# Graph attention and two transformer layers: projections on four quadrants of TensorE, values as the moving operand in the first turn, and key-value products computed one stage earlier

## The chip, the cores and the metric

The kernel runs on one core of one Trainium2 chip, all in fp32. The metric is the device time of one execution in microseconds (us); lower is better.

## What is computed

The input x has 32 sequences of 64 tokens with 256 features, and ctx has the same shape. Four blocks follow each other on x:

```python
# block 0 (cross attention over channels; C = 64 rows of a sequence)
q, k   = w_qk @ x, w_qk @ y              # y = ctx
energy = q_T_k                           # features x features, softmax, scaled by column sums
x      = x + relu(w_t @ (x - x_v @ attention) + b_t)
# blocks 1 and 2 (a transformer layer with 16 heads of 16)
h = layernorm(x); x = x + self_attention(h, mask) @ w_ao
h = layernorm(x); x = x + cross_attention(h, ctx, cross_mask) @ w_co
h = layernorm(x); x = x + gelu(h @ w1) @ w2
# block 3 (an RWKV-like layer: data-dependent mixing, decay, a recurrence
# over 64 tokens with 8x8 states per head, group norm, and a gated feed-forward)
```

In the attention of a layer, scores are masked, the row maximum is subtracted, exp is taken, and the product with the values is divided by the row's sum.

## The kernel before

Everything is in SBUF as 128-partition tiles, two sequences to a tile of tokens, and 4 groups of 4 such tiles. Each engine has its own instruction queue, written out in order by hand, and waits on semaphores. There are four parts.

**The gate stage** (`phase_a`, block 0) loops over 16 tiles of two sequences. On TensorE a step for tile t is `energy` of tile t+2 (L362), `project` of t+3, `turn_back` (L387), `read_out` of t+1 (L377) and `mix_out` (L393). `project` makes q and k of both sequences with a block-diagonal 128x128 weight: L348 for y (k's side), L349 for x, each 256 columns, into one PSUM bank, then the x-values by L352 into another. ScalarE's `copy_qk` (L439) copies q and k out when L349 is done; VectorE's `values` (L502) adds the bias to the x-values. SP loads x and y of a tile as two DMAs (`load`, L272 and L273). Its queue is in order: four reloads, four stores (L285), four reloads, and so on; a store waits for POOL's `add` (L330).

**The layers** (`phase_b`) are 8 turns, 4 groups times 2 layers. Turn 0 is written by `first_turn`, turns 1 to 6 are one loop over `turn`, and turn 7 is `last_turn`. Each turn has 8 attention tiles k (4 self, 4 cross) and in between the MLP of the turn before (`hidden` L1112, `pre`, `gelu` L1454, `mlp_out` L1126) and the entry projections of the turn after (`queries_in`, `keys_in`, both L944; `values_in`, L954). Turn 0 has no MLP of a turn before. One tile goes so:

- `scores` (PE, L1050) -> `mask` (DVE, L1715) -> `add_mask` (POOL, L788) -> `maximum` (DVE, L1722) -> `subtract` (DVE, L1727) -> `exps` (ACT, L1423)
- `probs_T` (PE, L1060, 8 transposes) -> `copy_pT` (ACT, L1428) -> `times_v` (PE, L1074): values are the stationary operand (32 columns, a pair of heads), probabilities move (64 columns); the result has heads' features in the partitions
- `row_sums` (DVE: a reduction over 1024 elements, L1733, and a reciprocal, L1735) -> `widen` (ACT, L1433) -> `inv_T` (PE, L1082, 2 transposes) -> `copy_inv` (ACT, L1438) -> `normalize` (DVE, L1740), which multiplies the product by the transposed 1/sum
- `out_project` (PE, L1095) -> `residual` (DVE, L1749 to L1756) -> `inv_std` (POOL, L793) -> `norm` (DVE, L1761)

The scores live in two buffers, so tile k+2 is masked after tile k's transposes. `cross_masks` (DVE, L1706 and L1707) prepares the cross mask and `norm_in` (DVE, L1689) the next turn's input once a turn.

**The last MLP with the recurrence's head** (`last_mlp_first_head`) runs the MLP of turn 7 together with block 3's projections for its first group: mixing, decay, k, v, r, g, and k and v turned to tokens (`to_tokens`). VectorE computes the key-value products of the first half of the features there (`key_value`, L2421, four instructions).

**Block 3** (`phase_c`) starts with `recurrence()`: 16 scans on VectorE (L3402), each followed by a product on POOL (L2612) and sums on TensorE, with the four key-value products of the second half of the features (L3392) between the first scans. `bonus` (PE, L2810) and `own_value` (DVE, L3407) give the diagonal term. Three periods and a last one follow.

```python
FIRST_PE, FIRST_DVE = {0: "b", 6: "n", 12: "l0 l1"}, {0: "k0", 1: "k1", 2: "k2", 3: "k3", 4: "b", 13: "s"}
```

says what stands behind which scan: `k0` to `k3` the products, `b` the diagonal term, `s` the next group's token shift.

## Time and profile before

| | |
|---|---|
| three runs | 1069.5, 1066.68, 1068.3 us; median 1068.3 |
| profiled execution | 1070.31 us, its span 1068.5 us, mean TensorE clock 0.981 |
| busy in the span | PE 983.8 (92%), DVE 837.1 (78%), ACT 558.6 (52%), POOL 435.6 (41%) |
| DMA | 41.10 MB, mean 38 GB/s |

Times inside the kernel are counted from the start of the span. PE is TensorE, DVE VectorE, ACT ScalarE, POOL GpSimd, SP the queue that issues the DMAs. A matmul in fp32 is two instructions in the profile. A merged row of the timeline gives the start of its first instruction and the time to the end of its last one, which can lie beside the next row's start. The gate stage ends at 96.7 us, turn 0 at about 178, turn 6 at about 658, turn 7 at 726.6, and block 3 begins at 792.5.

### The profile page before, as it was taken

To read this page: it belongs to the slowest core of one execution; us is meant where nothing else is said; L and a number is where in the kernel's file an instruction comes from. 1 tells how busy PE (TensorE), PEld (TensorE's weight loads), DVE (VectorE), ACT (ScalarE), POOL (GpSimd) and SP (SyncE) were. 2 spreads that over 40 slices of the span, in tenths; PEclk is the share of its full clock that TensorE was granted. 3 is DMA by queue.
4 is the path that set the end of the run, shared out by engine and by line. 5 is a ranking of instruction groups with operands and counts; after the bars stand their busy time and mean duration, and the time that the engine had idled before them with its cause. 6 is when DMAs were issued, how large, how long until landed. Compare 5 with 4: busy or idle time off the path is not lost. (4 is left out here: it accounts for less than half of the span.)

```text
span 1068.5 us, 24715 instructions
## 1 busy us (share of the span) xinstructions
PE 983.8 (92%) x9328; PEld 660.3 (62%) x9328; DVE 837.1 (78%) x1591; ACT 558.6 (52%) x1088; POOL 435.6 (41%) x383
## 2 busy tenths in 40 slices
PE   7998688999999999999999999998986988989877
PEld 5775566677677677677677677674552453554535
DVE  3775999977977877877977978785368898997965
ACT  4663464683683683683683783743412534415332
POOL 2112445434443444434444444342326527365250
PEclk9999999999999999999999999999998999999988
DMA  8230100000001002013000000030010010010010
GB/s 265 82 104 29 47 1 22 26 21 22 26 21 62 26 21 71 25 37 101 26 21 22 26 21 21 2 136 21 1 40 24 1 40 22 0 40 3 1 40 20
DMA packets 38003, 41.10 MB, mean 38 GB/s; under 512 B 8640, under 2 KB 33536, under 8 KB 37648
## 3 DMA queue, kind: packets, MB, share of 16 engines
q1 hardware_dynamic: 37776, 39.54, 11.7%
q8 instruction: 79, 1.29, 0.5%
q14 instruction: 20, 0.16, 0.0%
q0 software_dynamic: 128, 0.10, 0.0%
HBM read 31.25 MB, written 8.39 MB: 37 GB/s over the span
## 5 line engine op out<-in xcount | busy, mean ns | idle before, releaser
L788 POOL TENSOR_TENSOR head_area<-head_area,b_self_add 128x1024 f32<-128x1024 f32 x32 | 84.5, 2641 | 123.1 <-DVE head_area L1715 123.1
L2612 POOL TENSOR_TENSOR c_rs<-c_st,head_area 128x512 f32<-128x512 f32 x64 | 83.7, 1335 | 98.6 <-DVE c_st L3402 97.0
L788 POOL TENSOR_TENSOR head_area<-head_area 128x1024 f32<-128x1024 f32 x32 | 76.8, 2399 | 87.0 <-DVE head_area L1715 87.0
L1112 PE MATMUL ps<-b_hT_mlp,wl 128*128 128x512 f32 x224 | 105.6, 599 | 0.0
L1126 PE MATMUL ps<-w,b_act_g 128*128 128x256 f32 x448 | 102.9, 383 | 0.3 <-ACT b_act_g L1454 0.3
L1423 ACT ACTIVATE head_area<-head_area 128x1024 f32<-128x1024 f32 x64 | 68.0, 1063 | 51.9 <-DVE head_area L1727 51.8
L793 POOL TENSOR_TENSOR b_rstd<-b_var,minus_half 128x1 f32<-128x1 f32 x63 | 36.3, 577 | 142.8 <-DVE b_var L1756 142.8
L1126 PEld LDWEIGHTS ps<-w,b_act_g 128*128 128x128 f32 x448 | 82.8, 190 | 13.8 <-issue 2.2
L944 PE MATMUL ps<-head_area,wl 128*128 128x512 f32 x176 | 85.1, 607 | 3.1 <-DVE area L1698 2.5
L1428 ACT ACTIVATE head_area<-ps 128x512 f32<-128x512 f32 x128 | 69.3, 599 | 33.4 <-PE ps L1060 33.3
L1722 DVE TENSOR_REDUCE b_neg_max<-head_area 128x16 f32<-128x1024 f32 x64 | 77.7, 1213 | 11.5 <-POOL head_area L788 10.8
L1727 DVE TENSOR_TENSOR head_area<-head_area,b_neg_max 128x1024 f32<-128x1024 f32 x64 | 78.0, 1219 | 0.8
L1733 DVE TENSOR_REDUCE b_inv_sum<-head_area 128x16 f32<-128x1024 f32 x64 | 77.6, 1212 | 0.5 <-ACT head_area L1423 0.4
L3402 DVE TENSOR_TENSOR_SCAN c_st<-head_area,ps 128x512 f32<-128x512 f32 x64 | 73.4, 1202 | 2.6 <-ACT ps L3105 2.5
L1095 PE MATMUL ps<-wl,b_cT 128*128 128x256 f32 x252 | 68.2, 393 | 4.0 <-issue 2.4
L1060 PE MATMUL ps<-ident,head_area 128*128 128x128 f32 x512 | 66.9, 274 | 3.5 <-ACT head_area L1423 2.3
L1060 PEld LDWEIGHTS ps<-ident,head_area 128*128 128x128 f32 x512 | 58.4, 141 | 18.0 <-issue 12.4
L954 PE MATMUL ps<-wl,head_area 128*64 128x128 f32 x1024 | 64.2, 283 | 0.0
L954 PEld LDWEIGHTS ps<-wl,head_area 128*64 128x64 f32 x1024 | 58.4, 142 | 5.7 <-issue 4.8
L1112 PEld LDWEIGHTS ps<-b_hT_mlp,wl 128*128 128x128 f32 x224 | 39.7, 190 | 35.8 <-issue 35.1
L1438 ACT ACTIVATE head_area<-ps 128x256 f32<-128x256 f32 x64 | 24.4, 381 | 69.9 <-PE ps L1082 69.9
L1095 PEld LDWEIGHTS ps<-wl,b_cT 128*128 128x128 f32 x252 | 43.4, 189 | 14.1 <-issue 6.8
(294 smaller groups left out, 2153.0 us busy)
## 6 DMA issues: line engine op xcount, KB each, us to landing
head_area<-x_mid SPq DMA_DIRECT2D x9, 512.0 KB, 3.8
wl<-in_wl SPq DMA_DIRECT2D x4, 1024.0 KB, 6.4
head_area<-in_ctxT SPq DMA_DIRECT2D x8, 512.0 KB, 4.2
x_mid<-b_x_out SPq DMA_DIRECT2D x8, 512.0 KB, 3.5
area<-in_wc SPq DMA_DIRECT2D x1, 2336.0 KB, 8.3
a_x_in<-in_x SPq DMA_DIRECT2D x16, 128.0 KB, 2.8
a_y_in<-in_ctx SPq DMA_DIRECT2D x16, 128.0 KB, 3.5
w<-in_w SPq DMA_DIRECT2D x2, 1024.0 KB, 9.2
```

What stands on the lines that cost most here:

```text
L788: pool.tensor_tensor(t, t, m.unsqueeze(1).broadcast_to([P, NH, S]), ALU.add).then_inc(add_ok, 1)
L944: mm = pe.matmul(ps[:, YB + c, :], weight(name, k, first + c * P, first + (c + 1) * P), rhs[:, k, :], start=(k == 0), stop=(k == NC - 1))
L954: mm = pe.matmul(ps[odd * S:(odd + 1) * S, YB + half, b * P:(b + 1) * P], lhs[:, k, t:t + S], weight(name, k, odd * P, (odd + 1) * P), sta ...
L1060: mm = pe.transpose(ps[:, PT + half, i * P:(i + 1) * P], sc[:, k % 2, half, 2 * i:2 * i + 2, :].rearrange("q i k -> q (i k)"), w["ident"][ ...
L1095: mm = pe.matmul(ps[:, CO, OUT], cT[:, half, p * P:(p + 1) * P], weight(("ao", "co")[a], half), start=(half == 0), stop=(half == 1))
L1112: mm = pe.matmul(ps[:, YB + j % 2, :], weight("w1", k, j * P, (j + 1) * P), hT_mlp[:, k, :], start=(k == 0), stop=(k == NC - 1))
L1126: mm = pe.matmul(ps[:, YB + MLP_BANK[p], 0:D], act_g[:, j, p * P:(p + 1) * P], w["w2"][:, j, :], start=(j == 0), stop=(j == NJ - 1))
L1722: dve.tensor_reduce(neg_max[:, k % 2, :], t, AX, ALU.max, negate=True).then_inc(max_ok, 1)
L1727: dve.tensor_tensor(t, t, neg_max[:, k % 2, :].unsqueeze(2).broadcast_to([P, 2 * NPAIR, S]), ALU.add).then_inc(sub_ok, 1)
L1733: dve.tensor_reduce(inv_sum[:, k % 2, :], t, AX, ALU.add).then_inc(inv_ok, 1)
L2612: pool.tensor_tensor(rs[:, i % BUFS, :], st[:, i % 3, :], rF[:, i // RS, :], ALU.mult).then_inc(rs_ok, 1)
L3402: dve.tensor_tensor_scan(st[:, i % 3, :], decay[:, i // RS, :, :].rearrange("f b t -> f (b t)"), ps[:, VB[i % 4], :], 0.0, ALU.mult, ALU.a ...
```

## The change

Three parts. In the gate stage, `project` does four 64x64 matmuls of 256 columns, one for each quadrant of the array, q into the second half of the x-values' bank and k into the other bank. A quadrant off the diagonal takes sequence 1 to the partitions of sequence 0 and back, so y is loaded with its two sequences exchanged, in two DMAs. `copy_qk` waits for the x-values too, and `values` for `copy_qk`.

```diff
-                sp.dma_start(y_in[:, p, :], y).then_inc(ld_xy[p], 16)
+                for side in range(2):
+                    sp.dma_start(y_in[(1 - side) * S:(2 - side) * S, p, :], y[side * S:(side + 1) * S, :]).then_inc(ld_xy[p], 16)
...
-                pe.wait_ge(ld_xy[p], 32 // NP * (t - p) + 32)
+                pe.wait_ge(ld_xy[p], 48 // NP * (t - p) + 48)
                 after(pe, qk_ok, t)
-                pe.matmul(ps[:, PROJ, 0:D], w0[:, 0, :], y_in[:, p, :], start=True, stop=True)
-                pe.matmul(ps[:, PROJ, D:2 * D], w0[:, 0, :], x_in[:, p, :], start=True, stop=True).then_inc(proj_ps, 1)
                 after(pe, xvb_ok, t)
+                pe.sem_inc(proj_go, 1)
+                for side in range(2):
+                    h, other = slice(side * S, (side + 1) * S), slice((1 - side) * S, (2 - side) * S)
+                    pe.matmul(ps[h, XV, D:2 * D], w0[h, 0, h], x_in[h, p, :], start=True, stop=True)
+                    pe.matmul(ps[other, PROJ, 0:D], w0[h, 0, h], y_in[h, p, :], start=True, stop=True)
...
-                act.wait_ge(proj_ps, t + 1)
+                act.wait_ge(xv_ps, t + 1)
...
                 dve.wait_ge(xv_ps, t + 1)
+                dve.wait_ge(qk_ok, t + 1)
```

In turn 0 the probabilities become the stationary operand (64 columns) and the values move. The values of a pair of heads get two columns of ones (`VW = HD + 1`, set by four small memsets on POOL), so that the product brings the row sums with it. VectorE takes 1/sum of 16 columns and multiplies; the result, with tokens in the partitions, is transposed by `first_result_T` and copied by `first_copy_cT`. `row_sums`, `widen`, `copy_inv` and `normalize` are gone in turn 0; the later turns keep them.

```diff
+            def first_times_v(n, k):
...
+                    for i in range(NPAIR // 2):
+                        j = half * NPAIR // 2 + i
+                        for b in range(2):
+                            q = slice(b * S, (b + 1) * S)
+                            mm = pe.matmul(ps[q, CX, j * 2 * VW:(j + 1) * 2 * VW], pT[:, half, i, q], vP[a][:, 2 * p + b, j, :],
+                                           start=True, stop=True)
...
+            def first_result_T(n, k):
+                pe.wait_ge(inv_ok, 2 * tile(n, k) + 2)
+                for half in range(2):
+                    f = slice(half * P, (half + 1) * P)
+                    mm = pe.transpose(ps[:, CX, f], inv_wide[:, f], w["ident"][:, :])
...
+            def first_copy_cT(n, k):
+                p = k % NP
+                act.wait_ge(inv_ps, 2 * tile(n, k) + 2)
+                act.activation(cT[:, :, p * P:(p + 1) * P], ps[:, CX, CT].rearrange("f (h q) -> f h q", h=2), ACT.Copy).then_inc(c_ok, 1)
...
+            def first_normalize(n, k):
+                dve.wait_ge(inv_ps, 2 * tile(n, k) + 1)
+                pairs = ps[:, CX, 0:NH * VW].rearrange("q (j v) -> q j v", v=2 * VW)
+                inv = inv_sum[:, 0, :].rearrange("q (j o) -> q j o", o=2)
+                dve.reciprocal(inv, pairs[:, :, PW:2 * VW]).then_inc(inv_ok, 1)
+                dve.wait_ge(inv_ok, 2 * tile(n, k) + 1)
+                dve.tensor_tensor(inv_wide[:, :].rearrange("q (j o e) -> q j o e", o=2, e=HD), pairs[:, :, 0:PW].rearrange("q j (o e) -> q j o e", o=2),
+                                  inv.unsqueeze(3).broadcast_to([P, NPAIR, 2, HD]), ALU.mult).then_inc(inv_ok, 1)
```

With this the written orders of all three kinds of turn are new, on PE, ACT, DVE and POOL. In `turn` and `last_turn` nothing is added or removed. In turn 0, on VectorE, two tiles before and now (L1733 and L1735 are `row_sums`, L1740 `normalize`; L1764 is now `maximum`, L1769 `subtract`, L1757 `mask`, L1788 and L1790 `first_normalize`, L1799 to L1806 `residual`, L1811 `norm`). Before, tile 3's place:

```order
L1715 TENSOR_TENSOR head_area<-ps,head_area 128x1024
L1761 TENSOR_SCALAR b_xc<-b_x_cur,b_mv,b_rstd 128x256
L1733 TENSOR_REDUCE b_inv_sum<-head_area 128x16
L1735 RECIPROCAL b_inv_sum<-b_inv_sum 128x16
L1740 TENSOR_TENSOR b_cT<-ps,head_area 128x2x128
L1722 TENSOR_REDUCE b_neg_max<-head_area 128x16
L1727 TENSOR_TENSOR head_area<-head_area,b_neg_max 128x1024
```

and now, from `maximum(5)` to `maximum(7)`:

```order
L1764 TENSOR_REDUCE b_neg_max<-head_area 128x16
L1811 TENSOR_SCALAR b_xc<-b_x_cur,b_mv,b_rstd 128x256
L1769 TENSOR_TENSOR head_area<-head_area,b_neg_max 128x1024
L1788 RECIPROCAL b_inv_sum<-ps 128x16
L1790 TENSOR_TENSOR head_area<-ps,b_inv_sum 128x256
L1757 TENSOR_TENSOR head_area<-ps,head_area 128x1024
L1764 TENSOR_REDUCE b_neg_max<-head_area 128x16
L1769 TENSOR_TENSOR head_area<-head_area,b_neg_max 128x1024
L1757 TENSOR_TENSOR head_area<-ps,head_area 128x1024
L1788 RECIPROCAL b_inv_sum<-ps 128x16
L1790 TENSOR_TENSOR head_area<-ps,b_inv_sum 128x256
```

The reduction is gone, and a `mask` stands directly ahead of a `maximum`. `cross_masks` stood behind `mask(1)` and now stands behind `mask(3)`, and `norm_in` behind `mask(4)`.

In the middle turns, on ScalarE around the first gelu (L1423 and L1468 are `exps`, L1403 and L1448 `queries_in`, L1433 and L1478 `widen`, L1396 and L1441 `norm_out_mid`). Before:

```order
L1423 ACTIVATE head_area<-head_area 128x1024
L1433 ACTIVATE head_area<-b_inv_sum 128x256
L1403 ACTIVATE area<-ps,vl 128x512
L1454 ACT_TABLE_LOAD
L1454 ACTIVATE b_act_g<-b_act_g 128x2048
L1394 REGISTER_ALU
L1396 ACTIVATE head_area<-ps,vl 128x128 x2
```

and now:

```order
L1468 ACTIVATE head_area<-head_area 128x1024
L1504 ACT_TABLE_LOAD
L1504 ACTIVATE b_act_g<-b_act_g 128x2048
L1448 ACTIVATE area<-ps,vl 128x512
L1478 ACTIVATE head_area<-b_inv_sum 128x256
L1439 REGISTER_ALU
L1441 ACTIVATE head_area<-ps,vl 128x128 x2
```

The gelu moved ahead of `queries_in` and `widen`. On TensorE, `queries_mid(2)` moved from behind `probs_T(4)` to a place ahead of `keys_in(0)`, and `keys_ctx(0)` stands ahead of `last_project(0)` at the start of a turn. In turn 7, `hidden` and `mlp_out` are spread later: `mlp_out(3)` is now behind `inv_T(7)`.

The third part moves the four products of the second half of the features into the stage of the last MLP. Their buffer `kv2` then must be free before block 3: it shares the new tensor `early` with the layer weights that are no longer read by that time (`wl_early`, the first seven sets of columns; `wl_columns` finds the place).

```diff
-        FIRST_PE, FIRST_DVE = {0: "b", 6: "n", 12: "l0 l1"}, {0: "k0", 1: "k1", 2: "k2", 3: "k3", 4: "b", 13: "s"}
+        FIRST_PE, FIRST_DVE = {0: "b", 6: "n", 12: "l0 l1"}, {4: "b", 13: "s"}
...
-        kv = [kv1, sb("kv2", NP, RS * P)]
+        kv = [kv1, w["kv2"]]
...
+                key_value(0, 0)
+                key_value(0, 1)
+                key_value(0, 2)
+                key_value(0, 3)
+                next_norm()
+                key_value(1, 0)
+                key_value(1, 1)
                 own_weight()
-                next_norm()
                 result(0)
+                result(1)
+                key_value(1, 2)
+                key_value(1, 3)
                 gate()
-                result(1)
```

On VectorE, at the start of block 3, before (L3402 is the scan, L3392 the product):

```order
L3402 SCALAR_TENSOR_TENSOR c_st<-head_area,ps 128x512
L3392 TENSOR_TENSOR c_kv<-head_area 128x1024
L3402 SCALAR_TENSOR_TENSOR c_st<-head_area,ps 128x512
L3392 TENSOR_TENSOR c_kv<-head_area 128x1024
L3402 SCALAR_TENSOR_TENSOR c_st<-head_area,ps 128x512
L3407 TENSOR_TENSOR head_area<-ps,head_area 128x512 x2
L3402 SCALAR_TENSOR_TENSOR c_st<-head_area,ps 128x512 x9
```

and now, with the end of the stage ahead of it (L2462 is the product, L2408 `result`, L2438 `gate`, L3450 the scan):

```order
L2408 TENSOR_TENSOR b_x_out<-ps,b_x_mlp 128x256 x2
L2462 TENSOR_TENSOR early<-head_area 128x1024 x2
L2438 SCALAR_TENSOR_TENSOR head_area<-head_area,ps 128x512 x2
L2408 TENSOR_TENSOR b_x_out<-ps,b_x_mlp 128x256 x2
...
L3450 SCALAR_TENSOR_TENSOR c_st<-head_area,ps 128x512 x5
L3455 TENSOR_TENSOR head_area<-ps,head_area 128x512 x2
L3450 SCALAR_TENSOR_TENSOR c_st<-head_area,ps 128x512 x9
```

In the stage of the last MLP, TensorE's order changes too (`mlp_out(2)` goes behind the projections of r and g), and both gelus of ScalarE go behind the copies of k.

## Rows read from the trace of the kernel before

**Rows 1.** Busy time by stage: turn 0, a middle turn, turn 7, last MLP, recurrence
```profile
core 0: us, PE busy (x) PEld busy (x) DVE busy (x) ACT busy (x) POOL busy (x), PEclk, DMA share, GB/s
108.00:178.40 70.40, 55.00 (x829) 40.34 (x829) 65.12 (x118) 37.82 (x72) 37.44 (x31) 0.98 0.06 19
178.40:258.30 79.90, 79.41 (x919) 56.83 (x920) 66.42 (x130) 47.69 (x80) 34.37 (x30) 0.98 0.09 27
658.10:726.60 68.50, 64.89 (x766) 47.71 (x765) 57.80 (x118) 40.53 (x71) 26.23 (x24) 1.00 0.18 61
726.60:792.50 65.90, 61.52 (x200) 32.62 (x200) 29.76 (x60) 21.47 (x29) 14.48 (x14) 0.97 0.01 4
792.50:822.40 29.90, 19.18 (x103) 10.87 (x104) 28.76 (x28) 4.39 (x20) 23.00 (x16) 0.86 0.19 56
```
**Rows 2.** Timeline, gate stage, PE: start, us, instruction [idle before <-releaser]
```profile
41.75 1.14 PE L362 MATMUL ps<-a_qk 64*128 64x256 f32 x8
42.81 0.70 PE L348 MATMUL ps<-a_y_in,a_w 128*128 128x256 f32 x2
43.35 0.59 PE L349 MATMUL ps<-a_x_in,a_w 128*128 128x256 f32 x2
43.78 0.61 PE L352 MATMUL ps<-a_w,a_x_in 128*128 128x128 f32 x4
44.54 1.15 PE L377 MATMUL ps<-a_xv_n,a_att 128*64 128x65 f32 x32
46.25 1.14 PE L362 MATMUL ps<-a_qk 64*128 64x256 f32 x8
...
62.09 0.70 PE L348 MATMUL ps<-a_y_in,a_w 128*128 128x256 f32 x2 [1.21 <-DMA a_y_in<-in_ctx]
```
**Rows 3.** Timeline of the SP queue at tile 12, and L273's time to landing
```profile
58.30 0.43 SPq L273 DMA_DIRECT2D a_y_in<-in_ctx  x1
...
DMA to landing us min/median/max: 2.1/3.5/6.8
```
**Rows 4.** Timeline of DVE: turn 0, and L1707 in turn 0 and in turn 2
```profile
108.07 2.47 DVE L1707 TENSOR_SCALAR head_area<-head_area 128x256 f32<-128x256 f32 x1
...
144.38 1.21 DVE L1733 TENSOR_REDUCE b_inv_sum<-head_area 128x16 f32<-128x1024 f32 x1
145.62 0.25 DVE L1735 RECIPROCAL b_inv_sum<-b_inv_sum 128x16 f32<-128x16 f32 x1
...
273.73 0.29 DVE L1707 TENSOR_SCALAR head_area<-head_area 128x256 f32<-128x256 f32 x1
```
**Rows 5.** Timeline of PE in turn 0: `times_v` and `scores`
```profile
130.91 0.65 PE L1074 MATMUL ps<-head_area,area 128*32 128x64 f32 x32 [1.19 <-DVE b_cT L1740]
...
132.56 0.69 PE L1050 MATMUL ps<-head_area 32*64 32x128 f32 x32
```
**Rows 6.** Timeline of ACT, a middle turn: the first gelu
```profile
293.00 1.28 ACT L1454 ACT_TABLE_LOAD   x1
294.29 1.91 ACT L1454 ACTIVATE b_act_g<-b_act_g 128x2048 f32<-128x2048 f32 x1
```
**Rows 7.** Timeline of PE, end of turn 7
```profile
726.59 1.10 PE L2125 MATMUL ps<-wl,b_cT 128*128 128x256 f32 x4 [1.20 <-PEq L2036]
```
**Rows 8.** Timeline of DVE, stage of the last MLP: the four products
```profile
777.52 4.63 DVE L2421 TENSOR_TENSOR head_area<-head_area 128x1024 f32<-128x1024 f32 x4 [7.33 <-ACT head_area L2309]
```
**Rows 9.** Timeline of the recurrence: DVE, PE and POOL
```profile
794.71 1.20 DVE L3392 TENSOR_TENSOR c_kv<-head_area 128x1024 f32<-128x1024 f32 x1
795.83 1.22 DVE L3402 TENSOR_TENSOR_SCAN c_st<-head_area,ps 128x512 f32<-128x512 f32 x1
796.96 1.20 DVE L3392 TENSOR_TENSOR c_kv<-head_area 128x1024 f32<-128x1024 f32 x1
...
798.01 3.15 PE L2810 MATMUL ps<-head_area,area 128*128 128x512 f32 x4
...
806.16 11.55 POOL L2612 TENSOR_TENSOR c_rs<-c_st,head_area 128x512 f32<-128x512 f32 x9 [1.03 <-DVE c_st L3402]
```

More of the change, by code:

```diff
@@ new lines, in first_turn @@
+                queries_mid(n, 2)
+                norm_T_in(nxt, prev)
+                last_project(n, 4, prev)
+                probs_T(n, 4, nxt)
+                queries_in(nxt, 0)
+                first_times_v(n, 4)
+                next_scores(n, 4, nxt)
+                norm_T_mid(n, 3)
+                queries_in(nxt, 1)
+                first_result_T(n, 4)
+                probs_T(n, 5, nxt)
+                queries_mid(n, 3)
+                first_times_v(n, 5)
+                next_scores(n, 5, nxt)
@@ new lines, in first_turn, with last_turn @@
+                values_in(nxt, 1, prev)
+                first_result_T(n, 7)
+            def last_turn(n, prev, nxt):
+                keys_ctx(n, 0, prev)
+                probs_T(n, 0, nxt)
+                last_project(n, 0, prev)
+                times_v(n, 0)
+                next_scores(n, 0, nxt)
+                keys_ctx(n, 1, prev)
+                inv_T(n, 0)
+                values_ctx(n, 0)
+                last_project(n, 1, prev)
+                values_ctx(n, 1)
+                probs_T(n, 1, nxt)
@@ new lines, in turn @@
+                pre(prev, 4)
+                copy_inv(n, 2)
+                pre(prev, 5)
+                queries_mid(n, 1)
+                copy_pT(n, 3)
+                norm_out(0, nxt)
+                next_exps(n, 3, nxt)
+                gelu(prev, 0)
+                queries_in(nxt, 0)
+                widen(n, 3)
+                norm_out_mid(n, 2)
+                copy_inv(n, 3)
+                queries_in(nxt, 1)
+                queries_mid(n, 2)
+                copy_pT(n, 4)
+                next_exps(n, 4, nxt)
@@ new lines, in turn @@
+                keys(0, nxt, 0)
+                widen(n, 4)
+                copy_inv(n, 4)
+                norm_out_mid(n, 3)
+                keys(0, nxt, 1)
+                copy_pT(n, 5)
+                queries_mid(n, 3)
+                pre(prev, 6)
+                widen(n, 5)
+                pre(prev, 7)
+                next_exps(n, 5, nxt)
+                gelu(prev, 1)
+                copy_pT(n, 6)
+                widen(n, 6)
+                copy_inv(n, 5)
+                next_exps(n, 6, nxt)
@@ L1908, in first_turn @@
                 row_sums(n, 3)
+                norm_in(nxt if entry_of is None else entry_of)
                 normalize(n, 2)
```

841 lines of the change are left out of this document (391 added, 450 removed).

## The prediction

> **What bounds the kernel now.** I read the table of busy time by stage first [rows 1], then each engine's timeline inside a stage, since the page's average (PE 92%) mixes stages with different limits. A difference below 0.3% (3.2 us) can't be told from no change in a measurement of this kernel.
>
> In the gate stage (the first 96.7 us) TensorE works without a gap, 4.50 us a tile from one `energy` (L362) to the next, except where tile 12 waits 1.21 us for its y [rows 2]. In the first turn of the layers VectorE is busy for 65.12 of 70.40 us while TensorE is busy for 55.00 [rows 1]: VectorE sets the pace. In the six middle turns it is the reverse, TensorE 79.41 of 79.90, and the last turn is at 64.89 of 68.50. The stage that mixes the last MLP with the recurrence's head has TensorE at 61.52 of 65.90, VectorE at 29.76. In the recurrence VectorE is busy 28.76 of 29.90 us, TensorE 19.18. The later periods (246 us) are untouched by the diff.
>
> So a microsecond taken from VectorE counts in the first turn and in the recurrence, one taken from TensorE in the gate stage, and a new order of the middle turns can hardly win anything (0.5 us a turn) but can lose.
>
> **Part 1, quadrants.** Removed per tile: the two 128x128 by 256 matmuls L348 and L349, which take 0.97 us of TensorE (42.81 to 43.78) [rows 2]. Added: four 64x64 by 256. The price is not in the trace. From below, one 256-column matmul takes 0.43 us (L349, start to next start), and four quadrants that run side by side can't be faster. From above, `energy` has four 256-column matmuls on two halves of the array and takes 1.06 us to the next start. The nearest row is `scores` (L1050), which splits rows and columns both: sixteen matmuls of 128 columns on eight pieces, ideally 16 / 8 x 0.215 = 0.43 us, take 0.69 in their row, and about 0.16 of such a figure lies beside the next matmul (L349: 0.59 against 0.43) [rows 2, 5]. I take 0.60, so 0.37 us saved. The Trainium skill, "TensorEngine Tiling (Array Packing)", section Key Properties, says that a change of tiling mode drains TensorE, and the change adds one mode. The row bears on it: L348, behind a change of mode, takes 0.54 us to the next start and its twin L349 0.43, so a change costs 0.11 us, and that is inside the 0.60. Tiles 2 to 15 pay off, 14 x 0.37 = 5.2 us. The first two don't: ScalarE now copies q and k only after the x-values' matmuls too, which takes back what the quadrants save there.
>
> Against it stand the transfers. y comes as two DMAs, one more issue of 0.43 us on SP's queue, and the data lie there 2.1 us or more later [rows 3]. Ahead of the first matmul that is 0.5 us more. At tile 12 TensorE already waits; it arrives there 0.37 us earlier and y is complete up to 0.43 us later, so 0.8 us is lost. The reload of tile 8 has the same place behind the stores and starts without a gap only just, so 0.8 again. Sum of the part: 5.2 - 0.5 - 1.6 = **3.1 us faster**, bounds 6 (transfers don't matter) and 1 (the group takes 0.75).
>
> **Part 2, the first turn.** Per tile VectorE loses `row_sums`' reduction, 1.24 us from its start to the reciprocal's [rows 4]; the reciprocal and one multiply of 256 columns stay, with other operands. Eight tiles give 9.9 us of VectorE. ScalarE loses one small copy a tile, which is not on the path. How much of the 9.9 arrives? Three things stand in its place.
> First, TensorE: `first_times_v` has 16 matmuls with 64-column weights and 34 moving columns, where `times_v` (L1074) had 32-column weights and 64 moving columns, 0.65 us for its 32 instructions [rows 5]. The nearest row is L377, with 64-column weights too, 1.15 us for 32 [rows 2]. I take that, so 0.5 x 8 = 4 us more TensorE in a turn that has 15 us of slack.
> The Trainium skill, the same page, Instruction Overhead, states about 60 cycles for any short matmul; by that 34 columns would cost no more than 64 do, the 4 us would vanish, and the turn would be up to 2 us shorter.
> Second, the chain. Today 1/sum goes beside the transposes; now it waits for exp, transposes, copy and product, and then `first_result_T` and the copy of cT. With the order written in the diff, following VectorE's queue from row to row, the late maxima are hit: `mask(6)` is directly followed by `maximum(6)`, which needs POOL's mask in between (2.4 us).
> Third, `cross_masks` and `norm_in` now follow a `mask`, so that they run beside POOL's mask. What that costs is shown by L1707: 0.29 us alone, 2.47 us beside POOL [rows 4], some 2.2 us for each of the two. Today the 2.47 hides behind the wait for `maximum(1)`. The Trainium skill, "SBUF — State Buffer", explains such a pair as an exclusive lock on shared ports; the row agrees.
> I count 9.9 - 2.5 (exposed maximum, 2.4 and a start) - 2.2 (half of 4.4, the other half in idle time that the removal opens) - 1.2 (later residuals wait for the longer chain) = **4.0 us faster**, bounds 8 (only the maximum is exposed) and 1.
>
> **Part 3, middle and last turns.** No instruction is added or removed, only moved. A turn is 79.90 us long and TensorE fills it [rows 1]. I followed the new order by hand. The spot with least room is ScalarE's gelu: a table load and 1.91 us, 3.2 together [rows 6], now stand ahead of `queries_in`, `widen(3)` and `norm_out_mid(2)`, while TensorE's `queries_mid(2)` moved ahead of `probs_T(4)`. Behind `exps(4)` ScalarE then has 3.2 + 0.7 + 0.4 + 0.7 = 5.0 us of work, TensorE about 4.7 (transposes, two projections). That is a stall of 0 to 0.5 us a turn; against it keys_ctx now covers the turn's end. I take **0**, with 3 us loss and 1 us gain as bounds. In the last turn `mlp_out(3)` (3.5 us) moves behind the last `inv_T`, where TensorE idles 1.20 us now [rows 7]: **1 us faster**, bounds 3 and -1.
>
> **Part 4, products a stage ahead.** In the recurrence four key-value products of 1.12 us (794.71 to 795.83) leave VectorE [rows 9]: 4.5 us. Scans then follow each other at 1.13 us. POOL's product takes 1.28 us (11.55 / 9) and three buffers let it lag; with `own_value`'s 1.2 us and the shift's time between scans it catches up. TensorE's `bonus` (L2810, 3.15 us at the cold clock, first at 798.01) is gated by scan 1 and moves forward by about one product only, so `own_value` waits some 0.4 us. **4.1 us faster**, bounds 4.5 and 2.5. The products land in a stage where VectorE waits 7.33 us ahead of the first four [rows 8] and TensorE is the bound; eight products are 9 us. If the cover fails (values' tokens later than now), `result(3)` is late by at most 1.5 us; counted 0.
>
> **Sum.** 3.1 + 4.0 + 0 + 1 + 4.1 = 12.2 us off the profiled execution's 1070.31, whose span is 1068.5. The three runs have a median of 1068.3, 2.0 below it; taken off that, **1056 us**.
>
> **The rivals.**
> (a) *The first turn pays nearly in full and the transfers don't bite*: 8 instead of 4, 6 instead of 3.1, together 7 more: 1049. For it: the order was rewritten around the new durations. Against: the exposed maximum is in the order itself. 0.20.
> (b) *TensorE and the chain take the first turn back and the middle turns lose a little*: 1 instead of 4, and 0.5 us x 6: 1062. For it: TensorE's slack of 15 falls to 11 against 9.9 taken from VectorE, so both run near their limit. 0.18.
> (c) *Slower.* ScalarE's gelu block ends over 2 us after TensorE wants `queries_mid(2)`, in each of six turns. It decides from 12.2 / 6 = 2.0 us a turn; at 2.5 us it gives 1056 + 15 = 1071, at 3 us 1074. For it: TensorE has no slack to give there. Against: my count gives 0.5 at most. 0.05.
> (d) *The quadrants don't overlap* (they do not do what they say): four times 0.43 is 1.72 us, 0.75 more than today, x 14 = 10.5 slower in place of 3.1 faster: 1070, no change. Against: the rows of `energy` and `scores`, which overlap. 0.05.
> The forecast keeps 0.52.
>
> **Chances and range.** Forecast, (a) and (b) are faster by over 0.3% (below 1065.1); (d) is within 0.3%, (c) slower or just within. Faster 0.90, same 0.06, slower 0.04. The range takes in the bounds of the parts and half of (a): 1048 to 1063.
>
> **What would show it.** Tiles of the gate stage at 4.1 us, waits for y at tiles 8 and 12. In the first turn no L1733-like reduction, VectorE idle ahead of maximum(6), L1707's successor long beside POOL, the first middle turn some 7 us earlier. Middle turns at 79.9. Sixteen scans without a product between them, the recurrence's last `attention` 4 us nearer its start. The forecast is wrong if a tile stays at 4.5 us, if the middle period moves by over 0.5 us, or if VectorE's idle time in the first turn exceeds 10 us.

## The result, and the profile after

The changed kernel takes 1063.77 us in the median of 11 runs (1059.15 to 1066.76), the kernel before 1069.50 (11 runs, 1062.98 to 1075.45). The ratio is 0.9943, 95% interval [0.9924, 0.9963]: 4 to 8 us faster, and not the 12.2 that the sum had. A ratio is always the time over that of the kernel before, so below 1 is faster. The same kernel beside others later (`after_again`) had 1060.91 and 0.9917 [0.9894, 0.9940]. The profiled execution shown here took 1062.13 us, span 1060.2, where before had 1070.31 and 1068.5.

Busy time by stage of the kernel after: gate stage (to the first `scores`), first turn (to the second `probs_T` of turn 1, called its second transposes from here on), a middle turn, the last turn, last MLP, recurrence:

```profile
core 0: us, PE busy (x) PEld busy (x) DVE busy (x) ACT busy (x) POOL busy (x), PEclk, DMA share, GB/s
0.00:100.70 100.70, 80.56 (x922) 53.33 (x923) 57.83 (x151) 55.72 (x183) 21.06 (x32) 0.98 0.41 127
100.70:190.50 89.80, 79.26 (x1103) 61.18 (x1104) 72.99 (x135) 39.23 (x70) 42.54 (x35) 0.91 0.07 21
429.10:508.70 79.60, 79.08 (x930) 57.14 (x929) 65.74 (x128) 49.85 (x84) 35.71 (x29) 1.00 0.18 55
666.90:725.00 58.10, 56.05 (x624) 40.87 (x622) 46.66 (x98) 35.08 (x63) 21.69 (x20) 1.00 0.19 64
725.00:791.10 66.10, 61.67 (x200) 32.50 (x201) 33.51 (x64) 18.80 (x27) 14.54 (x14) 0.97 0.03 9
791.10:815.80 24.70, 16.64 (x103) 9.88 (x104) 23.57 (x23) 4.38 (x20) 18.69 (x15) 0.95 0.22 67
```

The same view of before, for the stretches that [rows 1] cut elsewhere:

```profile
0.00:96.70 96.70, 84.13 (x856) 61.89 (x856) 56.91 (x150) 56.26 (x183) 19.86 (x28) 1.00 0.42 132
96.70:188.00 91.30, 74.85 (x1102) 54.51 (x1103) 81.80 (x143) 42.31 (x78) 43.20 (x34) 0.94 0.07 21
666.00:726.60 60.60, 56.99 (x629) 41.64 (x627) 50.70 (x105) 36.12 (x64) 21.97 (x20) 1.00 0.20 66
792.50:821.70 29.20, 18.48 (x103) 10.66 (x104) 28.06 (x27) 4.39 (x20) 22.30 (x15) 0.87 0.19 58
```

Read the lengths in pairs. The recurrence is 4.5 us shorter and its VectorE lost just that (28.06 to 23.57). The last turn is 2.5 shorter. The first turn is 1.5 shorter although VectorE's busy time fell by 8.8 there, and TensorE's mean clock is lower (0.94 to 0.91). The gate stage is **4.0 us longer**, and its PE busy time fell with it: TensorE has less to do and waits. Who it waits for, in the gate stage of after:

```profile
PE ps L369 <- DMA a_y_in<-in_ctx: 5.1, 3, 2.4
PE ps L413 <- DVE a_diff L557: 2.8, 5, 1.1
PE ps L382 <- ACT a_qk L460: 2.7, 2, 2.0
```

and of before:

```profile
PE ps L393 <- DVE a_diff L535: 1.3, 4, 0.5
PE ps L348 <- DMA a_y_in<-in_ctx: 1.2, 1, 1.2
PE ps L362 <- ACT a_qk L439: 1.2, 1, 1.2
```

(total us, times, longest). The waits grew by 6.9 us: 3.9 for y, 1.5 for the copies of q and k, 1.5 for the difference. The longest is one that the prediction didn't have, at tile 4. TensorE's timeline of after at tile 4, and then a step without a wait:

```profile
27.62 0.40 PE L369 MATMUL ps<-a_x_in,a_w 64*64 64x256 f32 x1 [2.44 <-DMA a_y_in<-in_ctx]
28.24 1.23 PE L372 MATMUL ps<-a_w,a_x_in 128*128 128x128 f32 x4
29.82 1.93 PE L397 MATMUL ps<-a_xv_n,a_att 128*64 128x65 f32 x32
...
36.54 1.13 PE L382 MATMUL ps<-a_qk 64*128 64x256 f32 x8
37.60 0.43 PE L369 MATMUL ps<-a_x_in,a_w 64*64 64x256 f32 x1
38.20 0.71 PE L372 MATMUL ps<-a_w,a_x_in 128*128 128x128 f32 x4
38.74 0.38 PE L407 MATMUL ps<-ident,a_xr_t 128*128 128x128 f32 x2
...
40.77 1.14 PE L382 MATMUL ps<-a_qk 64*128 64x256 f32 x8
```

The quadrants do what they say: 37.60 to 38.20 is 0.60 us where the two matmuls took 0.97 [rows 2]. But L372 behind them now takes 0.54 to the next start, where L352 took 0.44, so a step is 4.23 us against 4.50: 0.27 saved, not 0.37. After the idle 2.44 us TensorE runs at its low clock: L397 takes 1.93 us there and 1.15 elsewhere.

SyncE's queue (start, us) shows why y is late. L284 and L272 load x, ahead of y. After:

```profile
1.74 1.18 SPq L286 DMA_DIRECT2D a_y_in<-in_ctx  x2
...
9.26 0.59 SPq L309 DMA_DIRECT2D early<-in_wl  x1
...
16.20 3.71 SPq L284 DMA_DIRECT2D a_x_in<-in_x  x1
20.01 1.16 SPq L286 DMA_DIRECT2D a_y_in<-in_ctx  x2
```

and before:

```profile
6.01 0.43 SPq L296 DMA_DIRECT2D wl<-in_wl  x1
...
14.18 3.22 SPq L272 DMA_DIRECT2D a_x_in<-in_x  x1
17.49 0.38 SPq L273 DMA_DIRECT2D a_y_in<-in_ctx  x1
```

A pair of issues holds the queue for 1.1 to 1.2 us. Four tiles push the first weights from 6.01 to 9.26, and the y of tile 4, issued at 20.01 and 20.70 where before issues it at 17.49, reaches TensorE at 27.62. From issue to landing it takes 6.9 us, and 6.8 in before: it is late because it is issued late. Whether the weights' bytes or their issues hold it up is not told by these rows; `late_weights` below bears on it.

### The profile page after: what moved, and what is told of

Same layout as the page of the kernel before. It is cut to its first block and busy times, and to the rows that moved or that the text cites. A ratio compares the mean times of both kernels' runs of the same rounds, so it can differ in the third digit from the quotient of the medians.

```text
span 1060.2 us, 24856 instructions
## 1 busy us (share of the span) xinstructions
PE 979.6 (92%) x9392; PEld 656.4 (62%) x9392; DVE 830.0 (78%) x1583; ACT 552.6 (52%) x1078; POOL 442.9 (42%) x387
## 3 DMA queue, kind: packets, MB, share of 16 engines
q1 hardware_dynamic: 38032, 39.55, 11.9%
q8 instruction: 84, 1.38, 0.5%
## 5 line engine op out<-in xcount | busy, mean ns | idle before, releaser
L815 POOL TENSOR_TENSOR b_rstd<-b_var,minus_half 128x1 f32<-128x1 f32 x63 | 52.1, 827 | 166.9 <-DVE b_var L1806 166.1
L2660 POOL TENSOR_TENSOR c_rs<-c_st,head_area 128x512 f32<-128x512 f32 x64 | 80.1, 1284 | 97.5 <-DVE c_st L3450 96.4
L810 POOL TENSOR_TENSOR head_area<-head_area,b_self_add 128x1024 f32<-128x1024 f32 x32 | 76.6, 2394 | 100.1 <-DVE head_area L1757 100.1
L1468 ACT ACTIVATE head_area<-head_area 128x1024 f32<-128x1024 f32 x64 | 67.9, 1060 | 50.6 <-DVE head_area L1769 50.5
L1764 DVE TENSOR_REDUCE b_neg_max<-head_area 128x16 f32<-128x1024 f32 x64 | 77.3, 1207 | 15.5 <-POOL head_area L810 15.3
L966 PE MATMUL ps<-head_area,early 128*128 128x512 f32 x176 | 84.5, 604 | 1.6 <-DVE b_x_out L1820 1.0
L1769 DVE TENSOR_TENSOR head_area<-head_area,b_neg_max 128x1024 f32<-128x1024 f32 x64 | 78.1, 1220 | 1.0
L3450 DVE TENSOR_TENSOR_SCAN c_st<-head_area,ps 128x512 f32<-128x512 f32 x64 | 72.9, 1199 | 2.6 <-ACT ps L3153 2.4
L1774 DVE TENSOR_REDUCE b_inv_sum<-head_area 128x16 f32<-128x1024 f32 x56 | 67.9, 1212 | 3.9 <-ACT head_area L1468 3.4
L976 PE MATMUL ps<-early,head_area 128*64 128x128 f32 x1024 | 65.4, 286 | 0.2 <-ACT head_area L1461 0.2
L976 PEld LDWEIGHTS ps<-early,head_area 128*64 128x64 f32 x1024 | 59.1, 144 | 5.2 <-issue 4.7
L1488 ACT ACTIVATE head_area<-ps 128x256 f32<-128x256 f32 x56 | 21.3, 381 | 55.4 <-PE ps L1104 54.9
L966 PEld LDWEIGHTS ps<-head_area,early 128*128 128x128 f32 x176 | 30.2, 190 | 27.6 <-issue 25.7
L2651 POOL TENSOR_TENSOR head_area<-head_area 128x512 f32<-128x512 f32 x30 | 36.4, 1227 | 24.3 <-DVE head_area L3423 23.8
```

What stands on the lines that cost most here:

```text
L810: pool.tensor_tensor(t, t, m.unsqueeze(1).broadcast_to([P, NH, S]), ALU.add).then_inc(add_ok, 1)
L966: mm = pe.matmul(ps[:, YB + c, :], weight(name, k, first + c * P, first + (c + 1) * P), rhs[:, k, :], start=(k == 0), stop=(k == NC - 1))
L976: mm = pe.matmul(ps[odd * S:(odd + 1) * S, YB + half, b * P:(b + 1) * P], lhs[:, k, t:t + S], weight(name, k, odd * P, (odd + 1) * P), sta ...
L1468: act.activation(t, t, ACT.Exp).then_inc(exp_ok, 1)
L1764: dve.tensor_reduce(neg_max[:, k % 2, :], t, AX, ALU.max, negate=True).then_inc(max_ok, 1)
L1769: dve.tensor_tensor(t, t, neg_max[:, k % 2, :].unsqueeze(2).broadcast_to([P, 2 * NPAIR, S]), ALU.add).then_inc(sub_ok, 1)
```

## The experiments

"First scores" is the first `scores` matmul, the end of the gate stage. One execution of a kernel says little about the whole (the 11 of the kernel before lie between 1062.98 and 1075.45 us), so totals are compared by ratios to the kernel before, and places by traces. First scores vary as well: in six traces with the old gate stage they come at 94.91 to 98.73 us (96.75 in before), in `after`, `after_again` and `gate_alone` at 99.35 to 100.69.

### Whose loss is it: the gate stage in and out

`gate_old` puts before's gate stage into the changed kernel, `gate_alone` puts the new one into the kernel before.

```diff
-                for side in range(2):
-                    sp.dma_start(y_in[(1 - side) * S:(2 - side) * S, p, :], y[side * S:(side + 1) * S, :]).then_inc(ld_xy[p], 16)
+                sp.dma_start(y_in[:, p, :], y).then_inc(ld_xy[p], 16)
...
-                    pe.matmul(ps[h, XV, D:2 * D], w0[h, 0, h], x_in[h, p, :], start=True, stop=True)
-                    pe.matmul(ps[other, PROJ, 0:D], w0[h, 0, h], y_in[h, p, :], start=True, stop=True)
+                pe.matmul(ps[:, PROJ, 0:D], w0[:, 0, :], y_in[:, p, :], start=True, stop=True)
+                pe.matmul(ps[:, PROJ, D:2 * D], w0[:, 0, :], x_in[:, p, :], start=True, stop=True).then_inc(proj_ps, 1)
```

> The changed kernel with the gate stage of before (two 128x128 matmuls, y in one DMA, not exchanged); layers and recurrence stay changed. In the traces the changed gate stage ends 3.9 us later than before's (first scores at 100.69 against 96.75). Theory A, the part made the gate stage a loss: first scores back near 96.8, whole kernel 4 to 5 us faster than the changed one, ratio to before about 0.989. Rival B, the 3.9 us are taken back in the first turn, where VectorE and TensorE wait anyway: less than 1.5 us faster than the changed kernel, ratio to before 0.993 to 0.995.

> The kernel before with the quadrants and the exchanged y alone. Theory A: slower by 3 to 5 us, ratio 1.003 to 1.005, with waits of project for y at tiles 4, 8 and 12. Rival B: within 1.5 us of before. My prediction's own step would have it 3.1 us faster, ratio 0.997.

Measured: `gate_old` 1055.67 us, 0.9850 [0.9821, 0.9879], first scores at 97.58. `gate_alone` 1074.93, 1.0046 [1.0023, 1.0068], first scores at 100.37, waits for y 4.4 us. The stage that was to win 3.1 us loses 5 us in the kernel before and 7 to 10 in the changed one (by its two ratios, 0.9917 and 0.9943, each difference with some 4 us of uncertainty). Theory A holds; nothing is taken back in the first turn.

### Which part of it: two ways around the late y

`pairs` loads y for two tiles in one DMA a side; `late_weights` moves the sets "out" and "hidden" to the end of the stage.

```diff
+                if p % 2 == 0:
...
+                    for side in range(2):
+                        sp.dma_start(y_in[(1 - side) * S:(2 - side) * S, p:p + 2, :], pair[side * S:(side + 1) * S, :, :]).then_inc(ld_xy[p + side], 16)
```
```diff
-            for s in SETS:
+            weights("first", "middle")
...
+            weights("out")
             for t in range(TILES - NP, TILES):
                 store(t, t % NP)
+            weights("hidden")
```

> The changed kernel with y loaded two tiles at a time, so that a tile costs SP's queue two issues again and not three; the quadrants stay. Theory A1, the stalls come from SP's queue (the pair of y issues takes 1.1 to 1.2 us where one took 0.43, so that the weights' loads start 3.2 us later and the y of tile 4 lands behind them): tile 4's wait of 2.44 us falls under 0.5, the waits at 8 and 12 (1.12, 1.57) under 0.8 each, first scores at or before 97, whole kernel 4 to 6 us faster than the changed one. Rival A2, the chain of the quadrants itself (q and k copied only behind the x-values' matmuls) costs the time: waits for y go, but TensorE waits for the copies and for a_diff instead, first scores stay at 99 or later, under 2 us faster.

> The changed kernel with the weight sets of the out projection and of the MLP (2.3 MB) loaded at the end of the gate stage and not at its start; three issues a tile stay. Theory A1a, tile 4's y waits behind those bytes: its wait of 2.44 us goes and with it the slow clock behind it (0.91 from 20 to 40 us), the waits at tiles 8 and 12 stay, first scores at 97 to 98, 2.5 to 4 us faster than the changed kernel. Rival A1b, it is the issue queue alone and not the bytes: tile 4 is still late by over 1.5 us, under 1.5 us faster.

`pairs`: 1064.01, 0.9934 [0.9909, 0.9960], first scores at 102.55. This attempt failed by its own making. A tile now waits for its neighbour's x too, and the first reload for a later tile comes later (18.73 against 16.20), so the waits for loads behind the first tile are 5.2 us, where the changed kernel has 5.1 for y. It decides nothing between A1 and A2.

`late_weights`: 1062.17, 0.9917 [0.9893, 0.9942]. Tile 4's wait is gone and the clock stays at 1.00 from 20 to 60 us, as A1a says, the waits at 8 and 12 stay (1.10, 1.20). But tile 4's y still takes 6.6 us from issue to landing. What changed is its issue, at 13.19 and not 20.01: five issues of weights ahead of it are gone, and the issue of x takes 0.35 us in place of 3.71. So the weights are shown as what delays it; whether by their bytes or by their time on the queue is not separated, since the run took away both. First scores come at 98.86 and not 97 to 98, as the wait for instructions ahead of them grew:

```profile
98.86 1.16 PE L1077 MATMUL ps<-area 32*64 32x128 f32 x32 [3.88 <-PEq L215]
```

where it was 2.38 in every kernel without these loads there. The gain of the whole is small and the interval holds 0.9943 too.

### All y loads in time

`ahead_late` and `ahead_mid` put the reload of tile t+6 ahead of the store of tile t; the large weights come at the stage's end, or right behind the last reload. `old_ahead` has the same reloads with the old stage.

```diff
             with sp.Fori(0, NG - 2) as it:
                 for p in range(NP):
-                    reload(NP * it + NP + p, p)
-                for p in range(NP):
+                    reload(NP * it + NP + p + 2, (p + 2) % NP)
                     store(NP * it + p, p)
```

> The changed kernel (quadrants, three issues a tile) with its loads issued in time: the reload of tile t+6 stands ahead of the store of tile t, where today four reloads stand behind four stores, and the weights of the out projection and the MLP come at the gate stage's end. Theory A3, the quadrants are worth what their matmuls save and y alone spoils it: no wait for y after the first tile, 5.1 us of waits gone and the slow clock behind tile 4 too, first scores at 94 to 95.5, and the whole kernel 2 to 3 us faster than the one with the old gate stage (1055.67 median, ratio 0.985). Rival B3, the chain of the quadrants (copies behind the x-values' matmuls, 2.7 us of waits for them at the start, 2.8 for a_diff) eats the rest: first scores at 96.5 or later, and no faster than with the old gate stage.

> The changed kernel with the old gate stage and the same earlier reloads (weights where they were). One wait of 1.4 us for y (tile 12) was left there: it goes, first scores from 97.58 to about 96.2, 0 to 1.5 us faster than the one with the old gate stage. If the stall is caused by a DMA queue and not by the order of issue, the wait stays.

> The changed kernel with the early reloads, and the out projection's and MLP's weights issued behind the last reload (about 56 us) and not at the gate stage's end, where the first scores then waited 3.88 us for TensorE's instructions instead of 2.38. Theory A4, that wait was made by the 2.3 MB in flight: back to 2.4, first scores at 93.5 to 94.5, 1 to 2 us faster than that kernel (ratio 0.986 to 0.987). Rival: the wait for instructions stays near 3.9, or the stores of x_mid are late; no gain.

| kernel | median us | ratio, 95% | waits for y | first scores |
|---|---|---|---|---|
| `ahead_late` | 1058.20 | 0.9887 [0.9864, 0.9910] | 0 | 95.21 (3.88 of it the wait for instructions) |
| `ahead_mid` | 1056.06 | 0.9873 [0.9851, 0.9895] | 0 | 95.06 (2.38) |
| `old_ahead` | 1056.72 | 0.9870 [0.9846, 0.9893] | 0.8 | 95.92 |

With every y in time the changed kernel gains about 5 us, and the quadrants then stand where the old stage stands. That is B3: they win nothing that can be measured (`old_ahead` has the large weights where they were, which is a difference beside the quadrants). TensorE's waits in the gate stage of `ahead_mid` show what eats their 0.27 us a tile:

```profile
PE ps L386 <- ACT a_qk L464: 2.7, 2, 2.0
PE ps L417 <- DVE a_diff L561: 2.6, 4, 1.1
```

Against 1.2 and 1.3 in the old stage that is 2.8 us. A4 is right about the instructions' wait (3.88 back to 2.38) and not about first scores: in that execution tile 1's `energy` still ran at the low clock (2.08 us against 1.13 in `both`, which has the same stage and first scores at 93.48).

### The y load alone, the quadrants alone

`before_split` changes nothing in the kernel before but splits the load of y, each half to its own place. `one_y` takes the split from the changed kernel: y comes in one DMA and isn't exchanged, so the gate pairs other sequences; the work is the same.

```diff
-                sp.dma_start(y_in[:, p, :], y).then_inc(ld_xy[p], 16)
+                for side in range(2):
+                    sp.dma_start(y_in[side * S:(side + 1) * S, p, :], y[side * S:(side + 1) * S, :]).then_inc(ld_xy[p], 16)
```

> The kernel before with nothing changed but that y comes in two DMAs of 64 rows, each to its own place (no exchange, no quadrants). Theory A5, the second issue makes the stalls (0.75 us more of SP a tile): the weights start 3 us later, waits for y at tiles 4, 8 and 12 add up to 4 us or more, where before has 1.2; first scores at 100 to 102 against 96.75, whole kernel 3 to 6 us slower than before, ratio 1.003 to 1.006. Rival B5, TensorE at 4.5 us a tile gives the loads the time that the quadrants' 4.23 does not: waits stay under 2 us, ratio 0.999 to 1.002.

> The changed kernel with y in one DMA and not exchanged, so that the quadrants pair the wrong sequences in the gate: the output is another, the work and its time the same. Theory A5: waits for y as in before or little more (tiles 8 and 12, under 2.5 us together, none at tile 4), first scores at 95 to 97, 3 to 6 us faster than the changed kernel, ratio 0.987 to 0.990. If the quadrants in themselves cost the time: first scores at 98 or later, ratio 0.992 and above.

`before_split`: 1077.82 us, 1.0057 [1.0032, 1.0082], first scores at 101.11. Its wait for y and its queue:

```profile
PE ps L349 <- DMA a_y_in<-in_ctx: 4.3, 3, 2.7
```
```profile
8.12 1.10 SPq L274 DMA_DIRECT2D a_y_in<-in_ctx  x2
9.26 0.59 SPq L297 DMA_DIRECT2D wl<-in_wl  x1
```

The weights start at 9.26 here too. `one_y`: 1055.92, 0.9857 [0.9827, 0.9886], first scores at 96.82, and

```profile
PE ps L368 <- DMA a_y_in<-in_ctx: 1.3, 2, 0.9
```

This settles which half of the part costs the time. The second DMA a tile costs the kernel before 6.1 us with no quadrant in it; taking it from the changed kernel gives all that `gate_old` gives (0.9857 against 0.9850, a difference with 4.5 us of uncertainty). With the pair `ahead_mid` and `old_ahead` (0.9873 against 0.9870) beside it, the quadrants are worth 0 within about 3 us. The wait at tile 4 isn't bound to the split alone: it is in all four traces with a split y and the weights ahead (1.60 to 2.70 us), but `first_old`, with one DMA, has it in its trace too (2.96 us, its y 8.3 us on the way), and the five others with the old stage have none (`before`, `gate_old`, `rec_alone`, `norm_only`, `order2`). The split makes frequent what is rare without it.

### The other parts, one upon the other

`rec_alone` has before's gate stage and all of before's turns: only the last MLP's stage and the recurrence are changed. `first_old` adds the new middle and last turns; `gate_old` adds the first turn.

```diff
-                first_times_v(n, 0)
+                times_v(n, 0)
+                inv_T(n, 0)
...
-                first_normalize(n, 0)
+                row_sums(n, 0)
+                normalize(n, 0)
```

> Old gate stage and all of the layers' turns as before, so that the stage of the last MLP and the recurrence alone are changed (products a stage ahead). My step says 4.1 us; the trace shows 4.55 at the head of the recurrence and 2.2 more behind it, where before has TensorE's clock at 0.84. If the 2.2 belong to the part: 6 to 7 us faster than before, ratio 0.994. If they are chance of the clock: 4 to 5, ratio 0.996. What is then left to the kernel with the old gate stage and the old first turn is the worth of the middle and last turns, 3 to 4 us by the traces where I took 1.

> Old gate stage and also the first turn of before on all engines (VectorE's row sums, ScalarE's widened inverse); middle turns, last turn and recurrence changed. Theory C, the new first turn wins little, since TensorE's clock falls to 0.75 in it (130 to 150 us) and VectorE waits 2.5 us twice for POOL's mask: from first scores to the second transposes of turn 1 88.63 us now, 91.3 in before: 1 to 3 us slower than the kernel with the old gate stage (ratio 0.986 to 0.988). Rival, the first turn pays my 4 us or more: ratio 0.989 or above.

| step | from ratio to ratio | us | forecast |
|---|---|---|---|
| products a stage ahead | 1 to 0.9946 [0.9927, 0.9964] | 5.8 | 4.1 |
| middle and last turns | to 0.9917 [0.9892, 0.9943] | 3.1 | 1 |
| first turn | to 0.9850 [0.9821, 0.9879] | 7.2 | 4.0 |
| gate stage | to 0.9943 [0.9924, 0.9963] | -9.9 | 3.1 |

Each step has an uncertainty of 3 to 4 us but the first (2). The last two rest on `gate_old`'s 0.9850, the lowest of four kernels whose gate stage loses nothing and whose first turn has no gain beyond the new one (`old_ahead` 0.9870, `norm_only` 0.9870, `one_y` 0.9857), so both are more likely too large than too small. For the products, the head of the recurrence, from the first scan to the first `attention`, takes 28.2, 30.2 and 30.3 us in the three traces that have the old one and 23.6 to 24.5 in the fourteen that have the new one: 5.7 us in the mean. The 2.2 us behind it in the first pair of traces are scatter of single executions (from first to last `attention` 211.0 us in before, with the clock low for 9.5 of them, 209.8 in `gate_alone`, which has the same recurrence, and 208.7 to 212.1 in those that have the new one). For the first turn, from first scores to the second transposes of turn 1, the old order takes 91.3, 93.1 and 89.7 us (before, `first_old`, `rec_alone`), the new one 89.8, 88.6 and 88.2 (after, `gate_old`, `old_ahead`): 2.5 us in the mean of three traces each.

### The first turn: two instructions behind a mask

In `gate_old` too TensorE's granted clock is at 0.75 of full speed from 130 to 150 us, and VectorE has these rows in the turn (start, us; L1742 is the second instruction of `cross_masks`, L1724 `norm_in`, and in the last row the `residual` waits 4.04 us for TensorE's `out_project`):

```profile
122.45 2.47 DVE L1742 TENSOR_SCALAR head_area<-head_area 128x256 f32<-128x256 f32 x1
132.33 3.82 DVE L1724 TENSOR_SCALAR xc_in<-head_area,mv_in,rstd_in 128x256 f32<-128x256 f32 x4
147.15 0.42 DVE L1792 TENSOR_TENSOR b_x_cur<-ps,head_area 128x256 f32<-128x256 f32 x1 [4.04 <-PE ps L1132]
```

TensorE's rows, same kernel, behind each of the first two (the transposes of a tile's `norm`):

```profile
129.57 0.65 PE L989 MATMUL ps<-ident,b_xc 128*128 128x128 f32 x2 [1.87 <-DVE b_xc L1804]
140.28 0.69 PE L989 MATMUL ps<-ident,b_xc 128*128 128x128 f32 x2 [1.97 <-DVE b_xc L1804]
```

`order2` moves both ahead of the mask that starts POOL; `norm_only` moves norm_in alone; `both` is `order2`'s first turn with `ahead_mid`'s gate stage.

```diff
                 next_subtract(n, 1, nxt)
-                next_mask(n, 1, nxt)
                 cross_masks(n)
+                next_mask(n, 1, nxt)
...
                 next_subtract(n, 2, nxt)
-                next_mask(n, 2, nxt)
                 norm_in(nxt if entry_of is None else entry_of)
+                next_mask(n, 2, nxt)
```

> The kernel with the old gate stage and, in VectorE's first turn, cross_masks and norm_in each moved ahead of a mask instead of behind it, so that they don't run beside POOL's mask (2.47 us against 0.29, and 4.6 us for four that should take 1.1). Theory C2, these 5 us delay the norms that TensorE waits for (1.87 and 1.97 us for b_xc), and that idle time lets its clock fall to 0.75 from 130 to 150: both waits under 1 us, clock at 0.9 or more there, from first scores to the second transposes of turn 1 3 to 5 us less than 88.6, ratio 0.981 to 0.983. Rival D2, the clock falls for its own reasons or the waits come from the residuals' chain: under 1.5 us gained.

> The kernel with the old gate stage, where of the two moves only norm_in goes ahead of its mask; cross_masks stays behind one. With both moves the first turn took 63.5 us from the second transposes on where it took 69.6, and the clock stayed at 1.0. Theory E, norm_in is the larger (3.8 us for four against 1.1) and stands ahead of the later wait, behind which the clock is at its low level to 150: 4 to 5 us of the 6. Rival F, both waits must go before the clock stays up: under 3 us, with 130 to 150 still below 0.9.

> Early reloads with the weights behind them, quadrants, and the reordered first turn: the sum of the two before, 5 us faster than the kernel with the old gate stage, ratio 0.978 to 0.981. If the first turn's gain is only taken at the slow clock of one arrangement, the two don't add up.

> The changed kernel once more, unaltered, as the control beside the three others on the same chip: ratio to before 0.992 to 0.996.

`order2`: **1051.45 us**, 0.9833 [0.9811, 0.9855]. `after_again`, the unaltered change, has 1060.91 beside it, but that difference holds the gate stage too; the kernel to compare with is `gate_old` (1055.67, 0.9850). In its trace the two rows are

```profile
120.01 0.28 DVE L1742 TENSOR_SCALAR head_area<-head_area 128x256 f32<-128x256 f32 x1
127.88 1.38 DVE L1724 TENSOR_SCALAR xc_in<-head_area,mv_in,rstd_in 128x256 f32<-128x256 f32 x4
```

and the stretches from 110 to 150 us

```profile
110.00:130.00 20.00, 16.39 (x291) 13.35 (x287) 19.49 (x48) 9.88 (x19) 10.39 (x9) 1.00 0.14 37
130.00:150.00 20.00, 17.94 (x266) 13.58 (x267) 14.89 (x27) 11.06 (x23) 11.85 (x9) 1.00 0.08 26
```

against those of `norm_only`:

```profile
110.00:130.00 20.00, 14.60 (x223) 11.90 (x220) 19.62 (x46) 9.46 (x17) 9.06 (x7) 0.91 0.12 34
130.00:150.00 20.00, 18.39 (x204) 14.27 (x201) 13.39 (x25) 9.12 (x19) 9.06 (x8) 0.84 0.08 27
```

and the waits of TensorE's transposes, in `order2` (the first is gone):

```profile
135.24 0.44 PE L989 MATMUL ps<-ident,b_xc 128*128 128x128 f32 x2 [1.15 <-DVE b_xc L1804]
```

and in `norm_only`:

```profile
126.90 0.69 PE L989 MATMUL ps<-ident,b_xc 128*128 128x128 f32 x2 [1.87 <-DVE b_xc L1804]
138.06 0.44 PE L989 MATMUL ps<-ident,b_xc 128*128 128x128 f32 x2 [1.15 <-DVE b_xc L1804]
```

From the second transposes of turn 0 to those of turn 1 `gate_old` takes 69.6 us, `norm_only` 69.1 (1056.54 us, 0.9870 [0.9841, 0.9899]), `order2` 63.5. This is no chance of one execution: the eight other traces with the new first turn and neither move take 69.0 to 69.7, and `both`, the other with both moves, 63.5. So F holds and E falls. norm_in in 1.38 us instead of 3.82 gave nothing in `norm_only`, where the first wait of 1.87 us is there and the clock is low right behind it. With both moved the first wait is gone, the second is 1.15 us and the clock stays up. The 6.1 us have two parts: 3.75 are there by the transposes behind the second wait (23.68 us after the start of the stretch in `gate_old`, 19.93 in `order2`), of the 4.6 us that VectorE was freed of, and 2.4 come between them and the next `probs_T` (6.67 against 4.25 us), which TensorE does at the low clock in `gate_old`. cross_masks moved alone was not run.

By whole runs the gain is less sure. Ratio to ratio it is 1.8 us from `gate_old` and 4.0 from `norm_only`, with some 4 us of uncertainty each; the two kernels with both moves have medians of 1051.45 and 1051.80, and `gate_old`, `one_y`, `norm_only` and `old_ahead`, which have at most one move and no loss in the gate stage, 1055.67 to 1056.72.

`both` has 1051.80, 0.9836 [0.9812, 0.9859]: first scores at 93.48 against 96.27, and yet no gain in the whole. What part of those 2.8 us the next stages take back is open: its execution had a colder recurrence (212.1 us from first to last `attention` against 209.4).

## Why the prediction failed

- **Part 1, the transfers.** The step that failed is "one more issue of 0.43 us on SP's queue". Only tile 0's and the reloads' own delay were counted. Two issues hold the queue 1.14 us where one held it 0.41; over the first four tiles that delays the weights by 3.25 us, and tile 4's y, which is issued behind them, by 2.5 us for its first half and 3.2 for its second: 2.44 us of idle TensorE and matmuls at the low clock behind it. The waits forecast at tiles 8 and 12 came (1.12 and 1.57 us, where before had none and 1.21; 0.8 more each was forecast). In place of 2.1 us of losses the second DMA costs 6.1 (`before_split`).
- **Part 1, the matmuls.** The 0.60 us of the group is right, and yet a tile takes 4.23 us and not the 4.1 that was to show it. The drain at a change of tiling mode, which the Trainium skill states ("TensorEngine Tiling (Array Packing)", Key Properties), was counted ahead of the group but not behind it, where L372 now takes 0.10 us more. And the later copies cost 1.5 us at the first tiles and 1.5 in waits for the difference. The prediction had ScalarE's later copies take back only what the first two tiles save. 5.2 us were forecast, nothing measurable arrives (`one_y` against `gate_old`).
- **Part 2.** 4.0 us forecast; 7.2 by the runs, 2.5 by the traces, so the size is not told better than its bounds 1 and 8. TensorE's cost was right: `first_times_v` takes 1.06 us to the next start against 0.59 for `times_v` [rows 5], 0.47 more where 0.5 was taken. The prediction's reading of the Trainium skill, the same page, Instruction Overhead, was wrong: the sentence compares numbers of moving columns. There the rows agree with it (32 instructions with 64-column weights take 1.06 us with 34 moving columns and 1.09 with 65, L397), but it doesn't make 64-column weights as cheap as the 32-column ones of `times_v`. Right too is the exposed maximum: `maximum(6)` waits 2.47 us for POOL's mask. So are cross_masks and norm_in beside POOL: 2.2 us each forecast, 2.2 and 2.4 measured (`gate_old` against `order2`). "Half of 4.4", 2.2 us, was not: by the traces the two cost 6.1, of which 2.4 lie in matmuls at the low clock, and the clock stood in no term. VectorE's idle time in the turn (its first `probs_T` to that of turn 1) went from 5.3 us to 11.9, over the 10 that the prediction named as a sign of being wrong.
- **Part 3.** The gelu block, rival (c), was no danger. Middle turns moved from 79.65 to 79.40 in the mean of six, inside the bounds. The last turn gave 2.5 us against 1, inside the bounds too. The runs say 3.1 for both together.
- **Part 4.** 4.1 forecast, 4.5 in the first pair of traces, 5.7 in the mean of all, 5.8 in the runs: the direction is right, the size a little low.
- Without the gate stage the parts were forecast at 9.1 us and gave 16.0 by `gate_old`'s ratio (13.9 by the medians, 12.0 by the spans of the two traces); the gate stage was forecast to win 3.1 and took 5 to 10 back. The two errors have opposite signs. The second is the larger, and that the first hides part of it is luck. The result has the time of rival (b), but not its reason: neither the first turn nor the middle turns lost.

## What to carry to other kernels

Count each added DMA in its queue from the first issue to the first consumer that is late, weights and other tiles included: here 0.73 us a tile became 6 us. Where TensorE's granted clock falls behind a wait, try the removal of all such waits together: in `norm_only`, with one of two left, the clock was still low, and the turn 0.5 us shorter and not 6. Place an operation of VectorE that POOL's work stretches ahead of the instruction that starts POOL, and not behind it.

## What the runs showed of the hardware

- A DMA of 64 rows isn't cheaper to issue than one of 128: SyncE's queue spends 0.48 us in the median on it (32 of them) and 0.41 on the whole tile (16), and 1.14 on two with what lies between.
- With 2.3 MB of weights issued at the end of the gate stage TensorE's wait for its instructions at the start of the next part was 3.88 us (`late_weights`, `ahead_late`), and 2.38 with the same loads issued earlier (`ahead_mid`) and in all others.
- An instruction's place alone can change its time ninefold: L1742 took 0.28 and 2.47 us, four times L1724 1.38 and 3.82. The Trainium skill, "SBUF — State Buffer", Who interferes with whom, describes an exclusive lock between VectorE and GpSimd for this; the rows agree with it.
- Behind its wait of 2.44 us in the gate stage TensorE ran at the lower of its two clocks (L397: 1.93 against 1.15 us), and in the first turn behind those of 1.87 and 1.97 us (clock 0.77 from 130 to 150 us in the changed kernel); in `order2`, whose longest wait from 110 to 150 us is 1.15 us, it stayed at the higher. The same wait of 1.87 us doesn't always do it at once: in `pairs`, `old_ahead`, `ahead_mid` and `one_y` the clock fell only at the next wait, of 3.59 or 3.60 us, and the turn took as long (69.0 to 69.2 us from second transposes to second transposes).
